# A graph layer on one core: the first part rearranged, and a sort whose last two merges stop early

## The chip, the cores and the metric

One core of a Trainium2 chip. The time is the device time of one execution in microseconds (us), and a kernel's time is the median of its runs. The trace gives one execution; its times count from the span's start.

## The reference

6250 nodes of 256 numbers and 100,000 edges (src, dst). Cut to what matters:

```python
xn = layernorm(x)
# graph part: a degree and a sum of rows over the edges
deg  = segment_sum(ones, src, n);  norm = rsqrt(1 + deg)
h    = norm * (xn @ W.T + bias)
gnn  = norm * (segment_sum(h[dst], src, n) + h)
# mixing part: linear attention with a gate
q, k, v = split(xn @ Wqkv);  k = softmax(k, over all nodes)
ctx  = k^T v per head;       out = q @ ctx
gate = sigmoid(gelu(layernorm(xn) * ln_g + ln_b) @ Wg1 + bg1) @ Wg2 + bg2)
x    = x + gnn + (out * gate) @ Wproj + bproj
# feed forward for about the half of the nodes with the largest weight
z    = layernorm(x);  w = z @ wr + br;  chosen = the 3124 largest w
x    = x + z  (and for the chosen: + w * (gelu(z @ w1 + b1) @ w2 + b2))
```

The edges reach the kernel in the order of dst. The sum needs them by src, and h[dst] is fetched row by row.

## The kernel before, in words

Node n is row n // 50 of window n % 50: 50 windows (NW) of 125 rows. An engine runs its own list of instructions in the written order and waits on semaphores; there is no scheduler. On VectorE nearly each instruction waits for the one before it (`step`).

**First part, to about 466 us.** VectorE makes from the edges row and window numbers, and counts the degrees in four chunks: `histogram(n)` first waits until TensorE has used up the chunk before (s_hist), then writes 50 comparisons with window numbers (L900) and 125 with row numbers (L904), and TensorE adds them up with 200 small matmuls (L592). The result is `deg`, from which `norm` comes (then s_normd), and a table of how many blocks of 256 edges each window needs: `first_block`, `end_block`, and `visits_due` for freeing. Each edge is packed into one key (window, row, column), and 128 x 1024 keys are sorted by a bitonic network on VectorE: a stage is a min (L975) and a max (L976). Stages within a partition for 768 of the columns come first (`early`, 36 stages, run by `lead` and then "open"), then those of the full width (9 + 10 of `local`, then the merges m = 1 to 7 over the partitions, with transposes at L998 and a sign product at L1002). Between them lie other duties of VectorE: the statistics of x (`rstd`, `nmr`, `r2`, then s_stats), `split_row`, and 25 `peek`s, each a maximum over a pair of windows of keys that TensorE has put into PSUM (`keys`; TensorE's pair i waits for peek i - 2). A peek inside the sort comes when `stages` reaches PEEK * (peeks - PEEK_FROM) - PEEK_LEAD. `stages` counts quarters of full-width stages: a stage on 768 columns counts 3, one on 1024 counts 4, and stages run by `lead` (open_keys=False) count nothing. When `stages` reaches KMAX_AT, VectorE splits the row of maxima into three bf16 parts and signals s_kmr.

ScalarE loads weights, computes the sum of each window's row (L440) for all 50 windows, then the sum of squares (L446) for all 50; x comes by SyncE in 5 loads of 10 windows (s_in0 to 4). Then it normalises each window (`scaled`), copies its transpose (`stored`) and makes the gate (`activated`, `gate_out`).

TensorE: `histogram(0)`, the transposes of the weights, `histogram(1)`, then over m = 0 to 49 `turn`, `hidden`, `keys`, `gate`, with the other two chunks ahead of m = 6 and 14 (HIST_AT). Then `main` (the rows h, of which the table in HBM is made: ScalarE `h_out`, GpSimd the subtraction L387, SyncE the stores), and from s_kmr on `keys_values` and `contexts` over 50 windows, with further `main`s in the first 17. Ahead of m = 28 (KEYS_AT) it waits for s_sortd and transposes the sorted keys (L732), of which VectorE makes columns and rows (s_tabs). After the last window it signals s_ctxd (L743).

**Second part, the gather loop.** GpSimd fetches rows of the table by column: 391 blocks of 256 edges, two gathers of 128 rows each (L403), in 23 rounds of 17 slots. It waits for s_freed for each block, and in the first round ahead of slot 14 for s_ctxd, for the last slots of `gath` also hold `qkv`. SyncE sees that a block has landed (s_arrived), waits until TensorE's count of visits reaches `visits_due`, and raises s_freed, which lets GpSimd run 15 blocks ahead; it also loads the column numbers of the next round. TensorE visits, per window w, the blocks first_block[w] to end_block[w] - 1 (`sums`, 2 matmuls L764 a visit), against a one-hot matrix that VectorE makes for each (`hots`, L1151, a ring of 8). In the same window lie turn_z, attention, up (L802), down (L812) and project (L787) on TensorE, `normed` on VectorE and the GELUs on ScalarE.

**Tail.** After the last window a search in 11 steps for the threshold, the sum for the chosen nodes and the stores.

Of the kernel before, what the change touches and what calls it, by code (L numbers as in the profile page):

```python
# [10 lines left out]
I32 = mybir.dt.int32  # L11
ALU = mybir.AluOpType
# [25 lines left out]
LAG = 2  # L38
HCH = 200
# [33 lines left out]
def gps_layer(nc, x, src, dst, W, bias, Wqkv, Wproj, bproj, ln_g, ln_b, Wg1, bg1, Wg2, bg2,  # L73
# [3 lines left out]
    with ctx:  # L77
# [205 lines left out]
        def _(sp):  # L283
# [125 lines left out]
        def _(a):  # L409
# [22 lines left out]
            a.wait_ge(s["wmain"], 16 * 9)  # L432
            for o in range(2):
                a.activation(WT[:, o, :], W_in[:, o, :], ACT.Square, accum_out=wss[:, o:o + 1]).then_inc(s["wss"], 1)
            for w in range(NW):
                if w % XCH == 0:
                    a.wait_ge(s_x[w // XCH], 32)
                if w >= SPILL:
                    a.wait_ge(s["bn"], w - SPILL + 1)
                a.activation(unused(xn)[:, w % SPILL, :], big_g[0:P, w, :], ACT.Identity, scale=-1.0 / C,  # L440
                             accum_out=mean_n[:, w:w + 1]).then_inc(s["bn"], 1)
            for w in range(NW):
                a.wait_ge(s["bn"], w + 1)
                if w >= SPILL:
                    a.wait_ge(s["bna"], w - SPILL + 1)
                a.activation(unused(h_s)[:, w % SPILL, :], big_g[0:P, w, :], ACT.Square, bias=mean_n[:, w:w + 1],  # L446
                             accum_out=var[:, w:w + 1]).then_inc(s["bna"], 1)
# [39 lines left out]
            a.wait_ge(s["bg1"], 1)  # L487
            for m in range(NW):
# [93 lines left out]
        def _(t):  # L582
# [35 lines left out]
            histogram(1)  # L618
# [128 lines left out]
            def sums(w, j, nth):  # L747
# [9 lines left out]
                with counted(t, f"sums{next(loops)}", first, end) as (q, upto):  # L757
                    made = q + (w + 1)
# [105 lines left out]
        def _(v):  # L864
# [19 lines left out]

            v.wait_ge(s["edges"], 64)
# [42 lines left out]

            v.wait_ge(s["wss"], 2)
            step(nc.vector.tensor_tensor(wun[:, :], b_col[:, :], b_col[:, :], ALU.mult))  # L930
            step(nc.vector.scalar_tensor_tensor(wss[:, :], wss[:, :], float(C), wun[:, :], ALU.mult, ALU.add))
            wss_i, wsc_i, wun_i = (of[:, :].bitcast(I32) for of in (wss, wsc, wun))
            step(nc.vector.tensor_scalar(wss_i, wss_i, 23, None, ALU.logical_shift_right))
            step(nc.vector.tensor_scalar(wss_i, wss_i, 2, None, ALU.add))
            step(nc.vector.tensor_scalar(wss_i, wss_i, 1, None, ALU.logical_shift_right))
            step(nc.vector.tensor_scalar(wsc_i, wss_i, -1.0, float(205 + TOP - 15), ALU.mult, ALU.add))
            step(nc.vector.tensor_scalar(wsc_i, wsc_i, 23, None, ALU.logical_shift_left))
            step(nc.vector.tensor_scalar(wun_i, wss_i, float(49 + 15 - TOP), None, ALU.add))
            step(nc.vector.tensor_scalar(wun_i, wun_i, 23, None, ALU.logical_shift_left))
            for o in range(2):  # L940
                step(nc.vector.tensor_scalar(W_in[:, o, :], W_in[:, o, :], wsc[:, o:o + 1], None, ALU.mult))
            nc.vector.tensor_tensor(b_col[:, :], b_col[:, :], wsc[:, :], ALU.mult).then_inc(s["wsc"], 1)

            for m in range(8):
                step(nc.vector.tensor_scalar(sign_i[:, m:m + 1], part_i[:, :], max(m - 1, 0), None, ALU.logical_shift_right))
            for m in range(8):
                if m == 0:
                    step(nc.vector.tensor_copy(sign_t[:, m:m + 1], sign_i[:, m:m + 1]))
                else:
                    step(nc.vector.tensor_scalar(sign_t[:, m:m + 1], sign_i[:, m:m + 1], 1, None, ALU.logical_shift_right))  # L950
                    step(nc.vector.tensor_tensor(sign_t[:, m:m + 1], sign_t[:, m:m + 1], sign_i[:, m:m + 1], ALU.bitwise_xor))
            step(nc.vector.tensor_scalar(sign_t[:, :], sign_t[:, :], 1, None, ALU.bitwise_and))
            step(nc.vector.tensor_copy(sign[:, :], sign_t[:, :]))
            step(nc.vector.tensor_scalar(sign[:, :], sign[:, :], -2.0, 1.0, ALU.mult, ALU.add))
# [69 lines left out]
            histogram(1)  # L1024
            v.wait_ge(s["kps"], 1)
# [16 lines left out]
            for _ in range(2):  # L1042
                peek()
# [5 lines left out]
            for _ in range(2):  # L1049
                peek()  # L1050
# [284 lines left out]
```

## Time and profile before

| | us |
|---|---|
| median of 3 runs (lowest, highest) | 1498.25 (1489.65, 1499.79) |
| the profiled execution | 1493.72 |
| its span, first to last instruction | 1492.0 |

A row's busy time is the sum of its instructions, and its idle time is what the engine waited just ahead of them. An engine that ends a wait is named after an arrow. POOL is GpSimd, DVE VectorE, ACT ScalarE, PE TensorE, SP SyncE; DVEq and the like are an engine's own queue of signals and transfers, PEld is TensorE's loading of weights, and PEclk the clock granted to TensorE as a share of full speed.

### The profile page before, as it was taken

The numbers are of one execution on the slowest core, as the hardware profiler recorded it, in microseconds if no ns is written. First come the engines' busy times: TensorE is split into PE (matmuls) and PEld (weight loads), VectorE is DVE, ScalarE is ACT, GpSimd is POOL, SyncE is SP. The second block draws the span as 40 slices with busy tenths as digits, with TensorE's granted clock in tenths as the row PEclk, the third lists the DMA queues.
The fourth block names the chain that finished last, engine by engine and source line by source line (L and its number), as shares of the span: only waits on it lengthen the run. The fifth ranks groups of instructions, "written<-read, shape, count | busy, mean of one in ns | idle before, by whom it ended". The sixth has DMA issues, their size and how long they took to land.

```text
span 1492.0 us, 29836 instructions
## 1 busy us (share of the span) xinstructions
PE 1146.9 (77%) x6606; PEld 868.8 (58%) x6607; DVE 1007.1 (68%) x3546; ACT 361.0 (24%) x1165; POOL 800.5 (54%) x851
## 2 busy tenths in 40 slices
PE   0367886789997888888777887878888777778843
PEld 0367775678885555556555555556565555555533
DVE  7888799999922666666655665656665556556657
ACT  0962354355421111111111111111111111111100
POOL 0000000154155777777777777777777777777700
PEclk9668998899999999999998998999999999999966
DMA  9000300022023444444443444444444344444305
GB/s 227 17 1 1 113 1 1 12 73 62 29 72 99 114 120 119 119 117 119 117 119 109 119 118 118 117 119 117 119 116 120 114 115 117 118 118 118 112 7 172
DMA packets 81194, 142.34 MB, mean 95 GB/s; under 512 B 30709, under 2 KB 53483, under 8 KB 80519
## 3 DMA queue, kind: packets, MB, share of 16 engines
q0 software_dynamic: 37536, 102.55, 23.8%
q1 hardware_dynamic: 28554, 24.55, 6.2%
q10 hardware_dynamic: 15054, 14.65, 3.3%
q8 instruction: 23, 0.38, 0.1%
q14 instruction: 27, 0.22, 0.0%
HBM read 126.43 MB, written 12.80 MB: 93 GB/s over the span
## 4 chain that ended last, share of the span: by engine, by line
DVE 25%; PE 23%; POOL 21%; issue 14%; DMA 9%; SPq 3%; ACT 2%; DVEq 1%; POOLq 1%; ACTq 0%
POOL gath L403 21%; DMA gath<-table,idx_stage 7%; PE bank L802 5%; PE bank L812 4%; PE bank L764 4%; DVE keyB L976 3%; DVE keyA L976 3%; DVE keyB L975 3%; DVE keyA L975 3%; DMA bg_t<-in_L_mix_bg 2%; DVE big_t L904 2%; SPq L337 2%; PE bank L779 2%; DVE big_g L1310 1%; PE bank L592 1%
## 5 line engine op out<-in xcount | busy, mean ns | idle before, releaser
L403 POOL DMA_INDIRECT gath<-table,idx_stage x782 | 748.9, 958 | 280.9 <-issue 226.0
L764 PE MATMUL bank<-gath,onehot 128*128 x880 | 272.8, 395 | 162.8 <-SPq L336 109.5
L1151 DVE TENSOR_SCALAR onehot<-iota_b,row_of,minus_row 128x128 bf16 x880 | 247.3, 334 | 133.9 <-issue 81.2
L764 PEld LDWEIGHTS bank<-gath,onehot 128*128 x880 | 84.5, 96 | 341.3 <-DVE onehot L1151 155.1
L802 PE MATMUL bank<-vv,w_sb 128*128 128x125 f32 x1600 | 212.1, 296 | 0.9 <-ACT vv L549 0.9
L802 PEld LDWEIGHTS bank<-vv,w_sb 128*128 128x128 f32 x1600 | 207.5, 213 | 2.6 <-ACT vv L549 1.7
L387 POOL TENSOR_TENSOR parts<-h_s,parts 125x256 f16<-125x256 f32 x50 | 46.8, 943 | 294.3 <-ACT parts L510 294.2
L812 PE MATMUL bank<-w_sb,keyB 128*125 128x256 f32 x800 | 181.0, 379 | 0.0
L563 ACT ACTIVATE WT<-bank,norm 125x256 f32<-125x256 f32 x50 | 23.7, 473 | 636.6 <-PE bank L771 624.9
L812 PEld LDWEIGHTS bank<-w_sb,keyB 128*125 128x125 f32 x800 | 146.3, 188 | 19.7
L555 ACT ACTIVATE keyB<-bank,b_sb 128x125 f32<-128x125 f32 x400 | 113.0, 366 | 184.4 <-PE bank L802 184.4
L1181 DVE SCALAR_TENSOR_TENSOR WT<-bank,norm,WT 125x256 f32<-125x256 f32 x50 | 24.2, 484 | 185.9 <-ACT WT L563 183.2
L592 PE MATMUL bank<-gath,big_t 125*128 125x50 bf16 x800 | 40.5, 230 | 55.6 <-DVE big_t L904 55.6
L779 PE MATMUL bank<-big_t,Wqc 128*128 (+1 forms) x400 | 72.1, 339 | 0.8 <-DVE Wqc L1247 0.8
L592 PEld LDWEIGHTS bank<-gath,big_t 125*128 125x128 bf16 x800 | 40.1, 120 | 55.9 <-DVE big_t L904 55.9
L779 PEld LDWEIGHTS bank<-big_t,Wqc 128*128 128x128 f32 x400 | 66.9, 252 | 1.3 <-DVE Wqc L1247 1.0
L904 DVE TENSOR_SCALAR big_t<-onehot 125x200 bf16<-125x200 bf16 x500 | 60.9, 216 | 0.0
L644 PE MATMUL bank<-big_t,gath 128*128 128x250 f32 x136 | 41.3, 457 | 24.3 <-DVE kpart L970 24.3
L787 PE MATMUL bank<-proj,W_in 128*125 128x256 f32 x200 | 52.9, 388 | 8.2 <-DVE W_in L1163 8.1
L691 PE MATMUL bank<-WT,big_t 128*125 128x256 f32 x200 | 52.3, 390 | 2.2 <-ACT parts L510 2.2
L699 PE MATMUL bank<-gath,big_t 128*125 128x256 f32 x200 | 51.5, 379 | 3.3 <-DVEq L991 3.3
L975 DVE TENSOR_TENSOR keyA<-keyB 128x512 f32<-128x512 f32 (+2 forms) x78 | 51.8, 664 | 2.4
(263 smaller groups left out, 1589.0 us busy)
## 6 DMA issues: line engine op xcount, KB each, us to landing
gath<-table,idx_stage POOLq DMA_INDIRECT x782, 2.7
parts<-table ACTq DMA_DIRECT2D x50, 125.0 KB
h_s<-in_x ACTq DMA_DIRECT2D x50, 125.0 KB
big_g<-in_x SPq DMA_DIRECT2D x5, 1120.0 KB
table<-parts SPq DMA_DIRECT2D x50, 112.0 KB
out<-big_g SPq DMA_DIRECT2D x10, 560.0 KB
w_sb<-in_L_ffn_w SPq DMA_DIRECT2D x2, 1024.0 KB
big_t<-w_sb SPq DMA_DIRECT2D x2, 1000.0 KB, 6.1
```

The source lines that it names most:

```text
L403: g.indirect_dma_start(out=gath[:, j, :], out_offset=None, in_=table[:, :], in_offset=bass.IndirectOffsetOnAxis(ap=idx_stage[:, j:j + 1], ...
L555: a.activation(hid[:, k, :], bank[5 + k // 4][:, (k % 4) * P:(k % 4 + 1) * P], ACT.Gelu_apprx_tanh, bias=b1_sb[:, k:k + 1]).then_inc(s["ge ...
L592: last = t.matmul(bank[3][:, 0:NW], hot_row[:, u // RUN, :, u % RUN], hot_win[:, u // RUN, :, u % RUN], start=False, stop=False, skip_grou ...
L764: last = t.matmul(bank[0][:, 0:PART], onehot_g[:, hot_slots, u * 128:(u + 1) * 128].rearrange("p a r -> p (a r)"), gath_g[:, slots, u * PA ...
L779: last = t.matmul(bank[1][:, half * P:(half + 1) * P], Wqc[:, c, half * 128:(half + 1) * 128], xnT[:, bass.ds(m, 1), c, :].rearrange("p a ...
L787: last = t.matmul(bank[3][0:P, 0:C], ogT[:, c, :], proj[:, c, :], start=c == 0, stop=c == 1)
L802: last = t.matmul(bank[5 + k // 4][:, (k % 4) * P:(k % 4 + 1) * P], w1_sb[:, c, k * 128:(k + 1) * 128], zT[:, c, :], start=c == 0, stop=c ...
L812: last = t.matmul(bank[7][0:P, 0:C], hid[:, k, :], w2_sb[:, k, :], start=k == 0, stop=k == HC - 1)
L904: last = nc.vector.tensor_scalar(hot_row[:, :, r, :], rows, float(r), None, ALU.is_equal)
L975: nc.vector.tensor_tensor(lo_out, lo_in, hi_in, ALU.min).then_inc(s["chain"], 1)
L976: nc.vector.tensor_tensor(hi_out, lo_in, hi_in, ALU.max).then_inc(s["chain"], 1)
L1151: last = nc.vector.tensor_scalar(onehot_g[:, slots, u * 128:(u + 1) * 128].rearrange("p a r -> p (a r)"), iota_b[:, :], row_of[:, bass.ds( ...
```

## The change

1. ScalarE does sums and squares per load of 10 windows instead of all sums first; the squares of W come after the third load instead of at the head.
2. VectorE's eight columns of signs are made as 8 wide operations ahead of the wait for the edges, instead of about 27 small ones behind the first histogram chunk. The scaling of W (from `wss`) moves behind the key building and two early stages.
3. The statistics go into the middle of the second histogram chunk, and s_stats is raised twice: for `rstd` and `nmr`, then for `r2`.
4. TensorE runs chunks 1, 2, 3 ahead of m = 3, 9, 15 (before: 1 ahead of the loop, 2 and 3 ahead of m = 6 and 14). VectorE has 26 instead of 16 of the 36 early stages in `lead`, laid between the chunks; peek 1 goes into chunk 2.
5. The block table comes after the remaining early stages. KEYS_AT is 24 instead of 28, PEEK_LEAD 20 instead of 12. KMAX_AT stays 297 (its formula does not hold PEEK_LEAD).
6. Merge m = 6 stops at distance 2^7 (its last seven stages go), merge m = 7 at 2^8 (its last two go). So keys are in order up to a short distance, and each window's range of blocks is widened: it starts at round(x) - 1 and ends behind round(x), where x is the count of edges up to there / 256, so that neighbours share two blocks and not one. The count of visits has 2 * m in place of m.

```diff
-PEEK_FROM, PEEK, PEEK_LEAD = 7, 17, 12
+PEEK_FROM, PEEK, PEEK_LEAD = 7, 17, 20
-HIST_AT = (6, 14)
-KEYS_AT = 28
+HIST_AT = (3, 9, 15)
+WSS_AT = 2
+KEYS_AT = 24
-LEADS = (4, 9, 16)
+LEADS = (2, 12, 17, 22, 26)
+MERGE_DOWN_TO = {6: 7, 7: 8}
...
@@ ScalarE
+            for q in range(NXL):
+                a.wait_ge(s_x[q], 32)
+                for w in range(q * XCH, (q + 1) * XCH):
...
+                for w in range(q * XCH, (q + 1) * XCH):
...
+                if q == WSS_AT:
+                    a.wait_ge(s["wmain"], 16 * 9)
...
             a.wait_ge(s["bg1"], 1)
+            a.wait_ge(s["stats"], 2)
...
@@ TensorE
-            histogram(1)
             t.wait_ge(s["wev"], 4)
...
-                    made = q + (w + 1)
+                    made = q + (2 * w + 1)
...
@@ VectorE
+            histogram(1, between=statistics)
+            lead(LEADS[0], LEADS[1])
+            peek()
+            histogram(2, between=peek)
+            peek()
             split_row(rows_h, "wtp", 1)
             v.sem_inc(s["rowsh"], 1)
+            lead(LEADS[1], LEADS[2])
             peek()
+            lead(LEADS[2], LEADS[3])
             histogram(3, between=peek)
+            peek()
+            lead(LEADS[3], LEADS[4])
+            peek()
...
+            for k, e in early[LEADS[4]:]:
+                local_stage(k, e, 0, EARLY)
...
-            step(nc.vector.tensor_scalar(til_i[:, :], scan[:, :], 1.0 / GEDGE, 0.5 / GEDGE - 0.5, ALU.mult, ALU.add))
+            step(nc.vector.tensor_scalar(til_i[:, :], scan[:, :], 1.0 / GEDGE, 0.5 / GEDGE - 1.0, ALU.mult, ALU.add))
+            step(nc.vector.tensor_scalar(til[:, :], til[:, :], 0.0, float(NBLK - 2), ALU.max, ALU.min))
-            step(nc.vector.tensor_scalar(end_block[:, :], til[0:1, :], 1.0, None, ALU.add))
+            step(nc.vector.tensor_scalar(end_block[:, :], til[0:1, :], 2.0, None, ALU.add))
...
-                for e in range(LOGF - 1, 6 if m == 7 else -1, -1):
+                for e in range(LOGF - 1, MERGE_DOWN_TO.get(m, 0) - 1, -1):
```

## Rows read from the trace of the kernel before

**Rows 1.** By stretch: us, busy us (count) of PE, PEld, DVE, ACT, POOL, PEclk, DMA, GB/s.

```profile
0.00:36.00 36.00, 0.61 (x10) 0.50 (x12) 27.56 (x193) 1.28 (x1) 2.48 (x15) 1.00 0.96 230
314.00:412.00 98.00, 97.16 (x530) 83.37 (x530) 95.61 (x114) 46.98 (x124) 32.62 (x35) 1.00 0.16 47
466.00:1418.00 952.00, 769.59 (x3985) 541.24 (x3985) 580.58 (x2143) 145.17 (x481) 722.18 (x754) 0.94 0.41 118
```

**Rows 2.** Timeline of GpSimd: start, us, instruction, in brackets idle time before it.

```profile
421.14 1.16 POOL L403 DMA_INDIRECT gath<-table,idx_stage  x1 [32.92 <-issue]
...
466.12 0.95 POOL L403 DMA_INDIRECT gath<-table,idx_stage  x1 [10.09 <-PE bank L743]
...
1417.09 0.95 POOL L403 DMA_INDIRECT gath<-table,idx_stage  x1 [0.30 <-issue]
```

**Rows 3.** GpSimd's gathers from 466 us on: shortest, median and longest in ns.

```profile
L403 POOL DMA_INDIRECT gath<-table,idx_stage x754: 942/946/1203, 466.1 to 1417.1; - x189
```

**Rows 4.** Timeline of TensorE.

```profile
314.44 1.13 PE L699 MATMUL bank<-gath,big_t 128*125 128x256 f32 x4 [3.26 <-DVEq L991]
...
412.31 1.09 PE L732 MATMUL bank<-ident,keyA 128*128 128x128 f32 x8 [0.70 <-DVEq L1114]
...
464.63 0.61 PE L743 MATMUL bank<-zeros_b,ident 128*128 128x129 f32 x4
...
513.35 0.17 PE L771 MATMUL bank<-zeros_b,ident_b 128*128 128x8 bf16 x1
...
531.23 0.17 PE L771 MATMUL bank<-zeros_b,ident_b 128*128 128x8 bf16 x1
...
1420.82 1.03 PE L764 MATMUL bank<-gath,onehot 128*128 x2 [2.85 <-SPq L336]
```

**Rows 5.** Timeline of VectorE in the first part.

```profile
41.77 0.16 DVE L930 TENSOR_TENSOR wun<-b_col 128x2 f32<-128x2 f32 x1 [6.21 <-ACT WT L434]
...
86.45 0.19 DVE L1032 TENSOR_SCALAR var<-var 125x50 f32<-125x50 f32 x1 [5.57 <-ACT h_s L446]
...
94.62 6.13 DVE L900 TENSOR_SCALAR gath<-onehot 125x200 bf16<-125x200 bf16 x50
...
166.00 0.21 DVE L1054 COPY deg<-bank 125x50 f32<-125x50 f32 x1 [4.68 <-PE bank L669]
...
205.62 0.69 DVE L975 TENSOR_TENSOR keyB<-keyA 128x512 f32<-128x512 f32 x1
...
282.62 0.68 DVE L970 TENSOR_REDUCE kpart<-bank 128x2 f32<-128x500 f32 x1
...
310.67 0.64 DVE L911 CAST rows_b<-lnb_wide 1x256 bf16<-1x256 f32 x1
...
411.51 0.68 DVE L976 TENSOR_TENSOR keyA<-keyB 128x512 f32<-128x512 f32 x1
```

**Rows 6.** VectorE by line and shape: 76 to 161 (two), 205.5 to 283, 293 to 391.

```profile
L904 DVE TENSOR_SCALAR big_t<-onehot 125x200 bf16<-125x200 bf16 x250 | 30.5, 214 | 0.0
...
L975 DVE TENSOR_TENSOR keyB<-keyA 128x384 f32<-128x384 f32 x8 | 4.5, 561 | 0.4
...
L975 DVE TENSOR_TENSOR keyA<-keyB 128x512 f32<-128x512 f32 x23 | 15.9, 691 | 0.7
...
L975 DVE TENSOR_TENSOR keyA<-keyB 128x512 f32<-128x512 f32 x22 | 19.1, 868 | 0.8
```

**Rows 7.** ScalarE by line, 40 to 90 us: count, busy us, mean ns, idle before.

```profile
L446 ACT ACTIVATE h_s<-big_g,mean_n 125x256 bf16<-125x256 f32 x50 | 24.6, 493 | 0.0
L440 ACT ACTIVATE xn<-big_g 125x256 bf16<-125x256 f32 x50 | 20.0, 400 | 0.0
```

**Rows 8.** From the page's costliest groups: TensorE's histogram matmuls, four chunks of 200.

```profile
L592 PE MATMUL bank<-gath,big_t 125*128 125x50 bf16 x800 | 40.5, 230 | 55.6 <-DVE big_t L904 55.6
```

**Rows 9.** By line in the gather loop, 466 to 1418 us: VectorE's onehots, TensorE's visits.

```profile
L1151 DVE TENSOR_SCALAR onehot<-iota_b,row_of,minus_row 128x128 bf16 x864 | 242.8, 334 | 130.6 <-issue 78.6 <-PE bank L764 45.8
...
L764 PE MATMUL bank<-gath,onehot 128*128 x878 | 271.8, 394 | 160.0 <-SPq L336 106.6 <-issue 26.1 <-DVE onehot L1151 24.1
```

More of the change, by code:

```diff
@@ L430, in unused @@
                 return of[:, :, :].rearrange("p a c -> p (a c)").bitcast(BF16).rearrange("p (a c) -> p a c", a=SPILL)
[L432 to L447, printed above, removed]
+            for q in range(NXL):
+                a.wait_ge(s_x[q], 32)
+                for w in range(q * XCH, (q + 1) * XCH):
+                    if w >= SPILL:
+                        a.wait_ge(s["bn"], w - SPILL + 1)
+                    a.activation(unused(xn)[:, w % SPILL, :], big_g[0:P, w, :], ACT.Identity, scale=-1.0 / C,
+                                 accum_out=mean_n[:, w:w + 1]).then_inc(s["bn"], 1)
+                for w in range(q * XCH, (q + 1) * XCH):
+                    a.wait_ge(s["bn"], w + 1)
+                    if w >= SPILL:
+                        a.wait_ge(s["bna"], w - SPILL + 1)
+                    a.activation(unused(h_s)[:, w % SPILL, :], big_g[0:P, w, :], ACT.Square, bias=mean_n[:, w:w + 1],
+                                 accum_out=var[:, w:w + 1]).then_inc(s["bna"], 1)
+                if q == WSS_AT:
+                    a.wait_ge(s["wmain"], 16 * 9)
+                    for o in range(2):
+                        a.activation(WT[:, o, :], W_in[:, o, :], ACT.Square, accum_out=wss[:, o:o + 1]).then_inc(s["wss"], 1)
             a.wait_ge(s["wmain"], 16 * 9)
@@ L927, in _ @@
             histogram(0)
[L929 to L954, printed above, removed]
             step(nc.vector.memset(keyA[:, :], EMPTY))
@@ L1039, in _ @@
-            inverse_sqrt(r2[:, :], nwt[:, 0, :], nwt[:, 1, :])
-            v.sem_inc(s["stats"], 1)
-            histogram(2)
-            for _ in range(2):
-                peek()
+            lead(0, LEADS[0])
+            v.wait_ge(s["wss"], 2)
+            step(nc.vector.tensor_tensor(wun[:, :], b_col[:, :], b_col[:, :], ALU.mult))
+            step(nc.vector.scalar_tensor_tensor(wss[:, :], wss[:, :], float(C), wun[:, :], ALU.mult, ALU.add))
+            wss_i, wsc_i, wun_i = (of[:, :].bitcast(I32) for of in (wss, wsc, wun))
@@ L1044, in _ @@
+            histogram(1, between=statistics)
[3 more added lines that the diff above has]
+            peek()
             split_row(rows_h, "wtp", 1)
             v.sem_inc(s["rowsh"], 1)
-            lead(LEADS[0], LEADS[1])
+            lead(LEADS[1], LEADS[2])
             peek()
+            lead(LEADS[2], LEADS[3])
             histogram(3, between=peek)
-            for _ in range(2):
-                peek()
-            lead(LEADS[1], LEADS[2])
+            peek()
@@ L1144, in hots @@
                 with counted(v, f"hots{next(loops)}", first, end) as (q, upto):
[L1145 removed]
+                    made = q + (2 * m + 1)
                     for value in (made, made % HOTS, q * GROUP):
```

64 lines of the change are left out of this document (41 added, 23 removed).

## The prediction

> **What bounds the kernel now.** I read the stretches first [rows 1]. In the gather loop (466 to 1418 us) GpSimd is busy 722 of 952 us, TensorE 770, VectorE 581, so shares do not name the limit; the gathers' own rows do. Gather 29 starts at 466.12 and gather 782 at 1417.09 [rows 2]: 753 steps of 1.263 us, against a median gather of 0.946 us and a gap of 0.30 us in front of each [rows 2, 3], 1.246 us. The difference, 12.8 us in all, is the only slack in 952 us. GpSimd is the bound of the loop, and the time is: start of gather 29, plus 951 us, plus the tail of 74 us.
>
> So the question is what starts gather 29. The first gather starts at 421.14, and 28 run; the 29th then waited 10.09 us for TensorE's L743 [rows 2], the end of the last `contexts` (s_ctxd, needed because the slots from 28 on hold `qkv`). That end is at 464.63 + 0.61 us [rows 4]. From 314.44 on TensorE does `keys_values` without a gap: 97.2 busy of 98 us [rows 1], with one wait of 0.70 us for the sorted keys at 412.31. At 314.44 it waited 3.26 us for VectorE's s_kmr (L991) [rows 4]. So the chain is: VectorE reaches the point KMAX_AT (310.67, where the row split begins, 3.7 us long) [rows 5], then 149 us of TensorE less 0.7, then the loop. The end of the sort (411.5) is only just on it.
>
> **Where KMAX_AT moves to.** I rebuild VectorE's order by durations.
>
> (a) Begin. The eight sign operations (0.2 us each) go into the wait for the edges and cost nothing. The first histogram chunk ends at 35.6 as before. The 6.21 us wait at 41.77 goes [rows 5]; key building (4.9 us) and two early stages (1.06 us each, from 0.56 + 0.55 overlapped, [rows 6]) follow, to 42.6.
>
> (b) ScalarE now works as x lands. Ten windows cost 10 x (0.400 + 0.493) = 8.9 us [rows 7]. x is 6.4 MB behind 0.8 MB of edges, and the stretch moved 230 GB/s [rows 1] over two queues; at 200 GB/s for this one, chunk 0 is there at 16 us and none is late. ScalarE: 16, 25, 34, 43 (`wss` at 44), 62 for s_bna instead of 86.3. Bounds: nothing lands before 12 (but `wmain` at 40.8 holds `wss`, so s_bna at 59.5), and 20 gives 66. I take 62.
>
> (c) VectorE: `wss` at 44.0, its block to 46.8, chunk two's first 50 + 62 comparisons (6.1 + 7.5 us, [rows 5, 6]) to 60.4, statistics (8.2 us, 86.45 to 94.62 before [rows 5]) 62 to 70.2, the other 63 comparisons to 77.8. Before, chunk two was ready at 75.9, but the statistics only at 94.6.
>
> (d) TensorE runs `histogram(1)` (10.1 us, [rows 8]) at m = 3. Steps m = 0 to 2 took 11.5 us after the statistics; with ScalarE held for the second s_stats they end at 79.3, the chunk at 89.5. VectorE has filled this with ten stages (88.4) and a peek, and waits 0.4. Chunk three 89.5 to 111.8, split, ten stages and peeks to 126.2, chunk four to 148.1, TensorE's part to 158.2. Four stages and two peeks (153.6) lie inside; about 4.7 us of wait stay, like the 4.68 before at 166.00. s_normd comes at 162.4 instead of 169.8: 7.4 us earlier, with ten more stages done.
>
> (e) Ten early stages are left instead of 20. They now look for TensorE's keys sooner (PEEK_LEAD 20); two of these waits come to 2.7 us. The 1.1 us wait for s_cntp goes, two small operations (0.4 us) come. Full-width stages begin at 187.1 instead of 205.6 [rows 5]: 18.5 us earlier.
>
> (f) But thresholds are counted in quarters of open stages. Early open stages give 3 quarters each: 60 before, 30 now. KMAX_AT is 297 as before, so it is reached at full stage (297 - 30) / 4 = 67 instead of 60. A full stage is 1.33 us uncontended: 205.62 to 282.62, less 10 peeks, 6 transposes and 3 sign products, is 61 us for 46. While GpSimd's `parts` subtractions run, the operations grow from 0.69 to 0.87 us on average [rows 6], and a stage to 1.6 to 1.9. Seven more stages at 1.75 are 12.3 us. Stage 52 comes at 273.3 by the shift; the last `keys` starts after it at 274.0 instead of 283.3 (9.3 earlier), and the subtractions move with it. Going on by those prices KMAX_AT is reached at 302.7, and `keys_values` begins at 306.5: **7.9 us earlier**. The nearest bounds: if the extra stages cost 1.33, TensorE's own path (9.3) is the limit; if (b) is at 66, 4 less. So 4 to 12.
>
> (g) The rest of the sort: nine stages go (seven in m = 6, two in m = 7), 11.3 + 2.7 us. m = 7 now falls under GpSimd's subtractions, + 3.5. The sort ends near 383. TensorE reaches m = 24 four steps of 2.29 us before m = 28: 411.6 - 9.2 - 7.9 = 394.5. The 0.7 us wait goes; VectorE stands idle 11 us. First gather near 403 instead of 421, gather 28 done near 439, then about 16 us wait for s_ctxd instead of 10. Most of what the sort saves is eaten here. Gather 29: **8.6 us earlier**.
>
> **What it adds in the loop.** Each window now ends two blocks after its rounded start and not one: visits are 389 + 2 x 50 = 489 instead of 440, 98 more matmuls and 98 more onehots of 0.334 us [rows 9]. TensorE unheld takes 17.9 us a window (513.35 to 531.23, nine visits [rows 4]); one visit more costs 0.83 (the visits there come so) to 0.98 us: 18.8. GpSimd needs 15.64 x 1.263 = 19.75. Cover stays, about 1 us a window, where L764's waits for arrivals are 106.6 us in all today [rows 9]. SP's `freed`: 15 blocks of lead, and the visit that frees a block comes 12 to 14 us later at worst, 6 blocks; only in window 1, where TensorE starts behind, a block 6 or 7 can hold the gather: 0 to 3 us, I take 1. Gathers beside onehots: if all 12.8 us of stretching came from today's 864 onehots, 98 more cost 1.5; I take 0.8. Tail: before the last block TensorE waited 2.85 us [rows 4], enough for one visit more and half a block of delay: 0.2.
>
> A rule against this change: the rows show that a gather's issue beside onehots is 942 ns at least, 946 at the median and 1203 at most [rows 3], so onehots hardly stretch it. The Trainium skill, "SBUF — State Buffer", section "SBUF: two separate sides", says that a VectorE operation in a two-port mode locks GpSimd out of writing descriptors. By that rule 98 onehots could cost up to 33 us more, by the rows 0 to 1.5; most of the trace speaks against it.
>
> **Sum.** -8.6 + 1 + 0.8 + 0.2 = -6.6 us. The profiled execution (1493.72, span 1492.0) would be 1487.1; the median of the runs shown is 1498.25, and 1498.25 - 6.6 = 1491.6. I say 1491.5. The case's own range: 1486 to 1496.
>
> **Rivals.**
> 1. The start of the gathers decides, because s_ctxd comes earlier than I think: the wait of 10.09 us vanishes and gather 29 follows 35 us after a first gather at 403, 27.7 us earlier; half of that, 14 to 28 us, is 1470 to 1484. For it: 33 us of VectorE work or waits go ahead of the sort's end. Against: TensorE is busy 97.2 of 98 us and nothing of `keys_values` gets shorter. 0.18; some 0.15 of it beyond 1%.
> 2. The extra visits make TensorE or GpSimd slower than 19.75 us a window. Place: the window loop; point: one visit more costs over 1.9 us in all, or every onehot blocks a gather for its 0.334 us (98 x 0.334 = 33 us, 1498.25 - 8.6 + 33 = 1522). TensorE 0.5 us over the gathers in 48 windows gives 1513. For it: TensorE's visits often wait for onehots (24.1 us [rows 9]), and 0.98 us a visit is VectorE's pace. Against: the 1 us of cover. 0.12.
> 3. The change does nothing: KMAX_AT 4 us earlier and 3 us held in window 1; 1496 to 1501. 0.18.
> My own case: 0.52.
>
> A few runs of this kernel tell about 1% (15 us) from no change. Faster by more 0.15, within 0.76, slower 0.09 (rival 2's milder half stays within). The range for 8 in 10 takes my case, rival 3, the nearer part of rival 1 and rival 2's begin: 1479 to 1504.
>
> **What would show it.** Statistics between 60 and 70 us inside chunk two; full-width stages from about 187; L991's release near 306; the sort's end near 383 with VectorE idle some 11 us ahead of L732; gather 1 near 403, gather 29 near 457.5 after a wait for L743 of about 16 us; 489 visits; 1.263 us a gather. I am wrong if gather 29 comes before 450 or after 463, if GpSimd's gaps grow past 0.30 us through the loop, or if L764's waits for arrivals vanish.

## The result, and the profile after

| | before | changed |
|---|---|---|
| median (lowest, highest), us | 1498.25 (1489.65, 1500.03) | 1488.3 (1485.61, 1490.97) |
| span of the profiled execution | 1492.0 | 1488.4 |

The ratio is 0.9948, with a 95% interval of 0.9928 to 0.9968: 0.5% faster, which counts as within 1%. The forecast was 1491.5. The medians lie 10.0 us apart, the spans of the two profiled executions 3.6: the one before was 4.5 us faster than its median, the changed one 1.9 us slower.

The stretches of the changed kernel that answer to [rows 1], with the same columns (us, busy us and count of PE, PEld, DVE, ACT, POOL, PEclk, DMA share, GB/s):

```profile
0.00:36.00 36.00, 0.70 (x12) 0.60 (x14) 29.30 (x202) 21.47 (x93) 2.48 (x15) 1.00 0.97 235
304.00:400.00 96.00, 96.00 (x514) 82.17 (x515) 79.50 (x88) 45.58 (x120) 36.44 (x34) 0.97 0.16 48
457.00:1419.00 962.00, 781.00 (x4081) 524.80 (x4081) 611.87 (x2238) 144.72 (x481) 727.33 (x754) 0.97 0.40 116
```

Its GpSimd timeline answers to [rows 2]. The gathers begin 18.2 us earlier, but gather 29, behind a wait of 19.2 us and no longer 10.1 for the contexts (L746, before L743), only 9.0 us earlier, and the last gather is no earlier at all:

```profile
402.98 1.16 POOL L405 DMA_INDIRECT gath<-table,idx_stage  x1 [22.40 <-issue]
...
457.13 0.95 POOL L405 DMA_INDIRECT gath<-table,idx_stage  x1 [19.22 <-PE bank L746]
...
482.81 0.94 POOL L405 DMA_INDIRECT gath<-table,idx_stage  x1 [0.99 <-SPq L341]
...
486.75 0.94 POOL L405 DMA_INDIRECT gath<-table,idx_stage  x1 [1.74 <-SPq L341]
...
542.46 0.94 POOL L405 DMA_INDIRECT gath<-table,idx_stage  x1 [2.90 <-SPq L341]
...
1417.61 0.95 POOL L405 DMA_INDIRECT gath<-table,idx_stage  x1 [0.30 <-issue]
```

The first part on VectorE and TensorE: the two timelines answer to [rows 5] and [rows 4]. The row split is at 300.62 (before 310.67), TensorE takes its signal at 303.89 (before 314.44), and VectorE is done with the sort at 381.1 and then stands:

```profile
43.59 0.16 DVE L1012 TENSOR_TENSOR wun<-b_col 128x2 f32<-128x2 f32 x1 [1.00 <-ACT WT L450]
...
61.43 0.19 DVE L1033 TENSOR_SCALAR var<-var 125x50 f32<-125x50 f32 x1 [0.18 <-ACT h_s L445]
...
156.80 0.21 DVE L1060 COPY deg<-bank 125x50 f32<-125x50 f32 x1 [4.83 <-PE bank L672]
...
184.25 0.69 DVE L960 TENSOR_TENSOR keyB<-keyA 128x512 f32<-128x512 f32 x1
...
300.62 0.28 DVE L923 CAST rows_b<-lnb_wide 1x256 bf16<-1x256 f32 x1
...
379.97 1.15 DVE L961 TENSOR_TENSOR keyA<-keyB 128x512 f32<-128x512 f32 x1
...
395.28 0.69 DVE L1127 COPY keyB<-bank 128x512 f32<-128x512 f32 x1 [14.15 <-PE bank L735]
```

```profile
288.87 0.37 PE L723 MATMUL bank<-ident,kmax 128*1 128x128 f32 x1 [3.19 <-DVE kmax L972]
...
303.89 2.07 PE L702 MATMUL bank<-gath,big_t 128*125 128x256 f32 x4 [3.64 <-DVEq L976]
```

The balance of the two spans, from gather 29 to the end: start -9.0; holds by s_freed beyond the usual gap +4.4 (4.7 against 0.3); the gathers' own durations and usual gaps over those 753 steps +5.1; from the last gather's start to the end 70.8 instead of 74.9, -4.1. Sum -3.6, the 1492.0 - 1488.4 seen.

### The profile page after: what moved, and what is told of

Its sections match the earlier page's. It is cut to its first block, busy times and chain, and to the rows that moved or that the text cites. A ratio compares the mean times of both kernels' runs of the same rounds, so it can differ in the third digit from the quotient of the medians.

```text
span 1488.4 us, 30493 instructions
## 1 busy us (share of the span) xinstructions
PE 1159.1 (78%) x6704; PEld 852.9 (57%) x6705; DVE 1027.4 (69%) x3612; ACT 360.8 (24%) x1165; POOL 809.8 (54%) x851
## 4 chain that ended last, share of the span: by engine, by line
PE 33%; DVE 26%; issue 14%; POOL 13%; DMA 5%; SPq 3%; DVEq 3%; ACT 3%; POOLq 0%; ACTq 0%
POOL gath L405 13%; PE bank L767 6%; PE bank L805 5%; PE bank L815 5%; DMA gath<-table,idx_stage 4%; PE bank L702 3%; PE bank L705 3%; DVE onehot L1159 3%; DVE big_t L916 3%; DVE keyA L961 2%; PE bank L694 2%; DVE keyB L961 2%; SPq L339 2%; DVE keyB L960 2%; DVE keyA L960 2%
## 5 line engine op out<-in xcount | busy, mean ns | idle before, releaser
L1159 DVE TENSOR_SCALAR onehot<-iota_b,row_of,minus_row 128x128 bf16 x978 | 277.3, 331 | 217.5 <-PE bank L767 110.5
L767 PE MATMUL bank<-gath,onehot 128*128 x978 | 301.0, 395 | 147.5 <-SPq L338 72.4
L767 PEld LDWEIGHTS bank<-gath,onehot 128*128 x978 | 93.9, 96 | 351.5 <-DVE onehot L1159 176.5
L389 POOL TENSOR_TENSOR parts<-h_s,parts 125x256 f16<-125x256 f32 x50 | 50.7, 1021 | 280.7 <-ACT parts L514 280.3
L805 PE MATMUL bank<-vv,w_sb 128*128 128x125 f32 x1600 | 198.4, 284 | 1.1 <-ACT vv L553 1.1
L805 PEld LDWEIGHTS bank<-vv,w_sb 128*128 128x128 f32 x1600 | 191.4, 199 | 3.0 <-ACT vv L553 1.7
L782 PE MATMUL bank<-big_t,Wqc 128*128 (+1 forms) x400 | 62.6, 306 | 0.8 <-DVE Wqc L1255 0.8
L782 PEld LDWEIGHTS bank<-big_t,Wqc 128*128 128x128 f32 x400 | 56.7, 218 | 1.5 <-DVE Wqc L1255 1.0
L960 DVE TENSOR_TENSOR keyB<-keyA 128x512 f32<-128x512 f32 (+2 forms) x78 | 51.3, 658 | 2.6
```

The costliest lines, as they stand in the source:

```text
L767: last = t.matmul(bank[0][:, 0:PART], onehot_g[:, hot_slots, u * 128:(u + 1) * 128].rearrange("p a r -> p (a r)"), gath_g[:, slots, u * PA ...
L782: last = t.matmul(bank[1][:, half * P:(half + 1) * P], Wqc[:, c, half * 128:(half + 1) * 128], xnT[:, bass.ds(m, 1), c, :].rearrange("p a ...
L805: last = t.matmul(bank[5 + k // 4][:, (k % 4) * P:(k % 4 + 1) * P], w1_sb[:, c, k * 128:(k + 1) * 128], zT[:, c, :], start=c == 0, stop=c ...
L960: nc.vector.tensor_tensor(lo_out, lo_in, hi_in, ALU.min).then_inc(s["chain"], 1)
L1159: last = nc.vector.tensor_scalar(onehot_g[:, slots, u * 128:(u + 1) * 128].rearrange("p a r -> p (a r)"), iota_b[:, :], row_of[:, bass.ds( ...
```

## The experiments

The table has one row per kernel: times of GpSimd's first, 29th and last gather (us from the span's start), holds beyond the gap of 0.30 us after gather 29, mean duration of the gathers from the 29th on, and the rest of the span behind the last gather's start. "Ratio" is against the kernel before on the same chip.

| kernel | median | ratio (95%) | first | 29th | last | holds | mean | rest |
|---|---|---|---|---|---|---|---|---|
| before | | | 421.1 | 466.1 | 1417.1 | 0.3 | 0.959 | 74.9 |
| changed | 1488.3 | 0.9948 (.9928-.9968) | 403.0 | 457.1 | 1417.6 | 4.7 | 0.966 | 70.8 |
| e1_narrow | 1484.18 | 0.9932 (.9910-.9954) | 402.0 | 456.2 | 1409.7 | 0 | 0.961 | 74.5 |
| e2_wide | 1501.15 | 1.0052 (1.0034-1.0071) | 421.2 | 466.0 | 1425.1 | 2.7 | 0.965 | 74.6 |
| e3_peek14 | 1469.44 | 0.9842 (.9825-.9860) | 392.2 | 437.1 | 1393.7 | 2.9 | 0.963 | 74.0 |
| e4_probe | 1524.44 | one run | 404.6 | 458.7 | 1450.1 | 36.8 | 0.965 | 72.5 |
| e10_narrow14 | 1468.7 | 0.9820 (.9795-.9845) | 402.1 | 437.7 | 1390.4 | 1.4 | 0.958 | 75.8 |
| e11_before14 | 1500.89 | 1.0028 (1.0012-1.0044) | 425.6 | 472.6 | 1425.7 | 0 | 0.961 | 74.3 |
| e12_before14 | 1486.35 | 0.9940 (.9922-.9957) | 428.6 | 463.8 | 1412.5 | 0 | 0.957 | 76.1 |
| **e9_peek12** | **1459.63** | **0.9766 (.9747-.9785)** | 392.1 | 427.4 | 1385.3 | 3.0 | 0.965 | 72.8 |

Theory A throughout: the time is the start of gather 29, plus 753 gathers of 1.26 us, plus the rest; and gather 29 is set by the row split (KMAX_AT), with the start of the gathers off the path. Its rivals stand with each run.

### Do the cut merges gain, and do the wide ranges cost?

e1_narrow is the changed kernel with finished merges and the old ranges; e2_wide is the kernel before with the wide ranges alone.

```diff
e1_narrow, against the changed kernel
-MERGE_DOWN_TO = {6: 7, 7: 8}
+MERGE_DOWN_TO = {7: 7}
...
-                    made = q + (2 * w + 1)
+                    made = q + (w + 1)
...
e2_wide, against the kernel before
-                    made = q + (w + 1)
+                    made = q + (2 * w + 1)
...
-            step(nc.vector.tensor_scalar(end_block[:, :], til[0:1, :], 1.0, None, ALU.add))
+            step(nc.vector.tensor_scalar(end_block[:, :], til[0:1, :], 2.0, None, ALU.add))
...
```

> The changed kernel with the merges finished as before (eight more full-width stages) and each window's range of blocks as narrow as before (440 visits). Theory A (TensorE's keys_values sets gather 29, the extra visits cost in the loop): the sort ends some 13 us later, near 394, just as TensorE comes to m = 24; gather 29 stays at 457 to 459; the holds of GpSimd by the freeing of blocks (0.99, 1.74 and 2.90 us) go, so the step from gather 29 to 782 goes from 960.5 back to about 952 to 956; the tail is again 74 to 75 us, since TensorE idles longer ahead of the last block. Span 1484 to 1488. Theory B (the unfinished merges bring the gain): slower than the changed kernel by some 10 us or more.

> The kernel before with nothing but the wider ranges (489 visits), its sort as it was. Theory A: first part unchanged (gather 29 at 466), GpSimd is held in the first windows for 3 to 6 us in all, the tail is about 4 us shorter because TensorE's last waits are short and its clock is up; span 1490 to 1496. Theory C (onehots block the gathers' descriptors, 0.33 us each for 98 more): the step from gather 29 to 782 grows by 30 us and the span is above 1515. Theory D (the growth of the gathers' durations by 5 us in the changed kernel belongs to the visits): the mean gather is 964 ns here too; if it is a matter of which VectorE operations of a window happen to meet a gather, it may be anything from 955 to 968.

Taking the cut merges away costs nothing: gather 29 comes at 456.16, 1 us earlier than in the changed kernel, because VectorE's 14.15 us of standing idle fill with stages; 2.02 us of it are left. The wide ranges cost more than I wrote (1499.7 as span, 1490 to 1496 said, and the shorter tail expected did not come): with everything ahead of gather 29 unchanged (465.98 against 466.12), the last gather of e2_wide is 8.0 us later, by 2.3 us of holds more and 4.5 us of longer gathers and the rest in gaps. The 7.2 to 1501.15 from the 1493.97 of the kernel before on that chip agree. The step from gather 29 to the last grew by 8.2 us and not by 30, so theory C is out. So part 6 of the change, cut merges and wide ranges together, gained nothing in this kernel: with PEEK = 17 the other parts alone (e1_narrow) are worth 0.68%, all of them 0.52%, two figures whose intervals overlap.

### Is it KMAX_AT that sets the time?

```diff
e3_peek14, against the changed kernel
-PEEK_FROM, PEEK, PEEK_LEAD = 7, 17, 20
+PEEK_FROM, PEEK, PEEK_LEAD = 7, 14, 20
-KEYS_AT = 24
+KEYS_AT = 28
```

> The changed kernel with the peeks 14 quarter stages apart instead of 17 (KMAX_AT then is 246 instead of 297, stage 54 instead of 67) and KEYS_AT 28. Theory A (VectorE's peeks and the KMAX_AT point pace TensorE, and its end of keys_values sets gather 29): the last keys of TensorE some 18 to 20 us earlier (near 252), s_kmr near 282 instead of 304, gather 29 near 437 to 440 instead of 457, span 1468 to 1472. Theory B (the end of the sort, or the start of the gathers, sets the end): no gain, since the sort ends where it did or a little later and TensorE's m = 28 is reached no earlier than m = 24 was.

Theory A holds, with a span of 1467.7, 0.3 us under its range. Peeks now come every 3.5 and not every 4.25 full stages, KMAX_AT falls from 297 to 246, TensorE takes the row split's signal at 283.9 instead of 303.9, and gather 29 moves by the same 20.0 us:

```profile
437.12 0.94 POOL L405 DMA_INDIRECT gath<-table,idx_stage  x1 [9.97 <-PE bank L746]
```

Two constants, PEEK and the KEYS_AT that goes with it, give more than the whole rearrangement. The wait of 9.97 us for the contexts says that TensorE still sets it, and how much is left until the 28 gathers do. This wait is only 9 us shorter than in the changed kernel, because the first gather moved as well, from 402.98 to 392.18: TensorE now comes to the sorted keys at 383.35 instead of 394.20.

### What does a VectorE operation cost a gather?

e4_probe put 40 comparisons of the onehot's form and then 40 sums of two f32 inputs (125 x 256) behind `hots(0)`; e8_probe put them the other way round ahead of it.

```diff
e8_probe, against the changed kernel
+            spin = keyB[:, 0:64].bitcast(BF16)
+            for _ in range(40):
+                step(nc.vector.tensor_tensor(keyB[0:P, 256:512], keyB[0:P, 512:768], keyB[0:P, 768:1024], ALU.add))
+            for _ in range(40):
+                step(nc.vector.tensor_scalar(spin, iota_b[:, :], row_of[:, 0:1], minus_row[:, 0:1],
+                                             ALU.subtract, ALU.is_equal))
             hots(0, bounds_of(0))
```

> The changed kernel with 80 more operations on VectorE in its wait for s_ctxd, beside the gathers from 403 to 438 us: first 40 of the onehot's form (128 x 128 bf16 from a constant tile and two scalars), then 40 sums of two 125 x 256 f32 tiles into a third. Theory C (a two-port operation locks GpSimd out): the gathers beside the first 40 stretch from 0.95 to 1.1 us or more each. Theory E (sums with two inputs in SBUF stretch the gathers, onehots do not): those beside the first 40 stay at 0.95, those beside the second 40 go to 1.07 to 1.2 us. If neither: all at 0.95. The span stays within 2 us, as the gathers after all wait for s_ctxd at 457.

> The changed kernel with 80 more VectorE operations between the first gather and the first onehot, where VectorE else waits 50 us: first 40 sums of two f32 inputs (125x256), then 40 comparisons of the onehot's form (128x128 bf16). Theory A (two-input sums delay a gather's issue, onehots do not): the gathers beside the first 40 take 1.05 to 1.10 us, those beside the second 40 0.94 to 0.96, as do those beside nothing. Theory B (it depends on VectorE being busy at all): both groups over 1.0 us. The span changes by less than 3 us against the changed kernel.

In e4_probe I had overlooked that `hots(0)` makes one onehot more than its ring of 8 holds. That last one waits for TensorE's first visit, so the probe began at 461.17, behind the contexts, and VectorE left the path's next step 34.7 us late:

```profile
460.71 0.54 DVE L1159 TENSOR_SCALAR onehot<-iota_b,row_of,minus_row 128x128 bf16 x2 [51.91 <-PE bank L767]
461.17 16.32 DVE L1246 TENSOR_SCALAR keyB<-iota_b,row_of,minus_row 128x128 bf16<-128x128 bf16 x40
477.52 18.36 DVE L1249 TENSOR_TENSOR keyB<-keyB 125x256 f32<-125x256 f32 x40
```

```profile
517.07 0.94 POOL L405 DMA_INDIRECT gath<-table,idx_stage  x1 [33.25 <-SPq L341]
```

Of the 34.7 us 33.3 stood at GpSimd as one wait: in the first windows next to no cover exists, which fits the place of the three holds of the changed kernel, 482 to 543. (Its 1524.44 us is no result on the price of an operation.) But the gathers ahead of that wait have the price: 13 of them beside the comparisons took 0.94 or 0.95 us, and the three wholly beside the sums, from 479.99 on, 1.07 or 1.08.

e8_probe, on a slower chip of which more below, gave the same price over more gathers. VectorE's rows and, under them, GpSimd's beside them:

```profile
400.87 18.36 DVE L1243 TENSOR_TENSOR keyB<-keyB 125x256 f32<-125x256 f32 x40 [0.43 <-DVE row_of L1133]
419.27 16.50 DVE L1245 TENSOR_SCALAR keyB<-iota_b,row_of,minus_row 128x128 bf16<-128x128 bf16 x40
```

```profile
406.64 0.99 POOL L405 DMA_INDIRECT gath<-table,idx_stage  x1 [0.30 <-issue]
407.94 1.08 POOL L405 DMA_INDIRECT gath<-table,idx_stage  x1 [0.31 <-issue]
409.32 1.07 POOL L405 DMA_INDIRECT gath<-table,idx_stage  x1 [0.30 <-SPq L341]
...
417.60 1.08 POOL L405 DMA_INDIRECT gath<-table,idx_stage  x1 [0.30 <-issue]
418.98 1.07 POOL L405 DMA_INDIRECT gath<-table,idx_stage  x1 [0.30 <-issue]
420.36 0.95 POOL L405 DMA_INDIRECT gath<-table,idx_stage  x1 [0.30 <-issue]
421.61 0.95 POOL L405 DMA_INDIRECT gath<-table,idx_stage  x1 [0.30 <-issue]
```

From 407.9 to 419 nine gathers of 1.07 or 1.08 us; from 420.36, beside the comparisons, 0.94 or 0.95, as beside nothing. So a onehot costs a gather nothing that can be seen, and sums of two SBUF inputs, back to back, cost 0.12 us a gather. The Trainium skill, "SBUF — State Buffer", section "SBUF: two separate sides", has a VectorE operation with two SBUF inputs share a port pair with GpSimd when GpSimd reads SBUF, and says that the loser "fully blocks". That such sums meet a gather, both probes bear out; they show no block for the length of the operation, for the sums took 0.46 us each, two or more met each gather, and it grew by 0.12.

Then why do 98 more onehots lengthen the gathers? In the loop I matched every gather of 1.12 us or more with the VectorE operations beside it. There are 14 of them before, and 10 to 19 in the four other kernels with narrow ranges (e1, e10, e11, e12); there are 42 in the changed kernel, and 33 to 40 in the four others with wide ones (e2, e3, e4, e9). The additional ones of the changed kernel lie beside L1178 and L1181 (`mixed`, 12, none with narrow ranges) and beside L1193 to L1201 (`normed`, 12, against 3 before): operations of two inputs that run in every window. Beside the onehots the wide ranges add nothing to what VectorE runs, so they must change when these chains run. That the chains lie closer to one another, and that this makes them dearer, is my reading; I have not tried it alone.

### Together with the narrow ranges, and how far down PEEK goes

```diff
e6_narrow14 and e10_narrow14, against e1_narrow
-PEEK_FROM, PEEK, PEEK_LEAD = 7, 17, 20
+PEEK_FROM, PEEK, PEEK_LEAD = 7, 14, 20
-KEYS_AT = 24
+KEYS_AT = 32
e5_peek11, against the changed kernel: PEEK = 11, KEYS_AT = 35
e9_peek12, against the changed kernel: PEEK = 12, KEYS_AT = 33
```

> The changed kernel with PEEK = 11 and KEYS_AT = 35. Theory A (gather 29 follows the later of two times: 149 to 153 us behind the row split, or 28 gathers behind the first one): KMAX_AT is 195, the last keys come once more earlier by up to 17 us, the last context ends near 420, and gather 29 is bound by the end of the sort: first gather near 390 to 392, gather 29 at 425 to 428 with no wait for the contexts; 1457 to 1462 us. Theory B (the peeks themselves are what costs, and fewer places for them leave TensorE's keys late): no gain over PEEK = 14, 1468 to 1472. Theory C (the loop gives it back, since TensorE starts a window behind): holds of over 3 us, 1463 to 1468.

> The changed kernel with finished merges and narrow ranges (440 visits), PEEK = 14 and KEYS_AT = 32. Theory A: the sort ends some 11 us later than with the merges cut (near 392), first gather near 402.5, gather 29 near 438 instead of 437.1; the loop then has no holds (2.9 us fewer) and some 3 us less of stretched gathers: 1464 to 1467 us. Theory B (the cut merges are what makes gather 29 early): 29 at 448 or later, 1476 or more.

> The kernel of e6_narrow14 once more, because in that call every kernel, the one before too, took some 46% longer, with ScalarE standing still for 12 to 21 us wherever gathers ran. Ahead of the gathers it did as expected (row split's signal used at 284.96 us, first gather at 402.70). On a chip without those halts, theory A: gather 29 near 438, no holds, 1464 to 1467 us. Theory B (the cut merges are what makes gather 29 early): gather 29 at 448 or later, 1476 or more.

> The changed kernel (cut merges, wide ranges) with PEEK = 12 and KEYS_AT = 33. Theory A (gather 29 is the later of TensorE's last context and 28 gathers behind the first): KMAX_AT is 212, keys_values begins near 275 and the contexts end near 428; the sort ends at 382 to 386, the first gather comes at 391 to 394, so both ways give 428 to 430 for gather 29, some 8 us earlier than e3_peek14. With its loop (2 to 3 us of holds, 0.963 us a gather) 1460 to 1464 us, against 1469.44 and 1468.7 of e3_peek14 and e10_narrow14. Theory B (with the peeks packed closer VectorE reaches TensorE's keys too early and waits, so that the sort ends later by as much): first gather at 397 or later, 1465 to 1470.

e5 to e8 ran on one chip on which all kernels took 46% longer: the kernel before 2178.62 us, e5_peek11 2149.08, e6_narrow14 2151.33, e7_before14 2182.2, e8_probe 2176.68. Their whole times say nothing on the theories, but ahead of the first gather their traces are like those of the other chips (row split's signal in e6_narrow14 at 284.96, first gather at 402.70), and those parts count. The last section shows the difference. In e5_peek11 the signal came at 269.2 and the sorted keys were waited for until 387.2, with a first gather at 397.2. The sort ended at 387.1, 4 us later than with PEEK = 12 below (383.2), and its gathers began 5.1 us later, so 11 looks worse than 12; its whole time on an ordinary chip was not measured. e7_before14, at a ratio of 1.0025, already showed what e11_before14 shows below.

e10_narrow14 did what A says, 1.7 us above its range: gather 29 at 437.72 behind a wait of 0.63 us. It is now bound by the 28 gathers behind a first one at 402. That is where the cut merges begin to be worth something: e9_peek12, which keeps them, starts its gathers at 392.12; TensorE takes the row split's signal at 274.19, waits only 0.60 us for the sorted keys at 383.30, and is done at 424.8, so gather 29 has no wait:

```profile
392.12 1.17 POOL L405 DMA_INDIRECT gath<-table,idx_stage  x1 [43.39 <-issue]
...
424.85 0.94 POOL L405 DMA_INDIRECT gath<-table,idx_stage  x1 [0.30 <-PE bank L746]
...
427.35 0.95 POOL L405 DMA_INDIRECT gath<-table,idx_stage  x1 [0.30 <-issue]
...
456.67 0.94 POOL L405 DMA_INDIRECT gath<-table,idx_stage  x1 [1.64 <-SPq L341]
```

```profile
274.19 1.03 PE L702 MATMUL bank<-gath,big_t 128*125 128x256 f32 x4
...
383.30 1.09 PE L735 MATMUL bank<-ident,keyA 128*128 128x128 f32 x8 [0.60 <-DVEq L1122]
```

At 1459.63 us, just below A's range, it beats both kernels, 2.3% under the one before. Against e10_narrow14 it pays 5 us in the loop for wide ranges and gets 10 for the earlier first gather. PEEK = 12 with finished merges was not run; as the sort of e10_narrow14 ended at 393.0 and its gathers, which already set gather 29, began at 402, I estimate that it would gain next to nothing over e10_narrow14.

### Does the kernel before gain from PEEK = 14 as well?

```diff
e7_before14 and e11_before14, against the kernel before
-PEEK_FROM, PEEK, PEEK_LEAD = 7, 17, 12
+PEEK_FROM, PEEK, PEEK_LEAD = 7, 14, 12
e12_before14, besides
-KEYS_AT = 28
+KEYS_AT = 37
```

> The kernel before with PEEK = 14 alone. Theory A: the row split comes 18 to 20 us earlier (near 291), the contexts end near 446, but the sort still ends at 411.5 and the first gather comes at 421, so gather 29 is at 456.3 without a wait for the contexts: 10 us earlier than before, 1482 to 1486 us; so the rearrangement, worth 8 us with PEEK = 17, is worth some 15 with 14. Theory B (the gain of PEEK = 14 is one of the changed kernel's order only): same as before, 1492 to 1496.

> The kernel of e7_before14 once more, for the same reason. Ahead of the gathers it showed keys_values begun at 295.9 (before: 314.4), the sorted keys waited for 19.8 us and a first gather at 422.5. Theory A: gather 29 near 457.6 without a wait for the contexts, 8.5 us earlier than before: 1484 to 1488 us. Theory B (the wait for the sorted keys is only moved into TensorE's path: 29 stays at 463 or later): 1491 to 1496. Theory C (PEEK = 14 gives the kernel before all 20 us): 1473 to 1476.

> The kernel before with PEEK = 14 and KEYS_AT = 37 instead of 28, so that TensorE does nine more windows of keys_values before it needs the sorted keys. Theory A (in e11_before14 the 20 us of KMAX_AT were lost because TensorE stood at m = 28 for the sorted keys and had 22 windows of 2.29 us left behind them): no wait for the keys, contexts end near 446 to 450, first gather 421 to 425, gather 29 at 457 to 461 bound by the 28 gathers: 1485 to 1490 us, so the change is worth 18 to 25 us with PEEK = 14 on both sides. Theory B (VectorE or ScalarE is late for another reason): gather 29 at 466 or later, 1496 to 1501.

In e11_before14 none of my three ranges held; it was slower than before by 0.28%. Theory B had the mechanism, the wait moved into TensorE's path, but not its price. TensorE has its signal 16.6 us earlier (297.86), but stands at m = 28 for the sorted keys:

```profile
415.94 1.97 PE L732 MATMUL bank<-ident,keyA 128*128 128x128 f32 x8 [19.24 <-DVEq L1114]
```

Behind that wait there are still 22 windows of 2.29 us, and gather 29 comes at 472.59. I had treated the sort's end and the row split as two ends of which the later counts; they are two entries into one TensorE queue, and what stands behind KEYS_AT has to be added to the later of them. With KEYS_AT = 37 (e12_before14) the wait is gone, the contexts end at 452.1, and gather 29 comes at 463.82, bound by the 28 gathers behind a first one at 428.58: 1486.35 us, in A's range, though contexts and gathers came 2 to 4 us later than A's places for them (the profiled execution took 1490.44). The first gather is 7.4 us later than before. The sort itself is hardly longer (163.0 us of full-width operations, before 162.2); its last stage is 6.0 us later (417.5 for 411.5) because its first is 6.4 us later (212.0 for 205.6). Ahead of it VectorE waits 1.5 us longer for `wss` (7.68 instead of 6.21; 5.54 to 7.09 in the other kernels with the old order), 2.1 longer for `deg` (6.8 instead of 4.7, in e7, e11 and e12 alike) and 1.9 more for TensorE's keys at the peeks, of which one more lies there. The other 1.5 us is TensorE, which comes to the sorted keys that much after they are done. With PEEK = 14 the change is worth the step from 0.9940 (e12_before14) to 0.9842 (e3_peek14), or to 0.9820 without part 6 (e10_narrow14), with PEEK = 17 from 1 to 0.9948; these ratios come from different chips.

## Why the prediction was right, by its steps

The path was named rightly: row split, TensorE's `keys_values` and `contexts`, 28 gathers off the path, then GpSimd's pace. (TensorE's part is 150.8 us by [rows 4], 314.44 to 465.24, and not 149; only its change enters the sum.) Most times of the first part met theirs within 2.5 us: `wss` 43.6 (44.0), statistics 61.4 (62), the wait for `deg` 4.83 (4.7), first gather 402.98 (403), gather 29 457.13 (457.5).

- **Full-width stages** began at 184.25, not 187.1. The two peeks' waits in (e) were 1.8 us and not 2.7, and `deg` came at 156.8, not 158.2.
- **Row split, (f).** 300.62 instead of 302.7. That the counting of quarters eats about half of the 21 us gained was right; the gain at TensorE was 10.5 us instead of 7.9. I had not seen that TensorE would wait 3.19 us for the last peek's maximum at 288.87. It did not delay the signal, which TensorE again awaited (3.64 us), but it has a part in the next point.
- **From there to gather 29** 153.2 us instead of 151.7, so that the start was 9.0 us earlier for 8.6 said. The sum had no term for TensorE's clock. After the two stands, 3.19 us before 288.87 and 3.64 before 303.89, the clock granted from 304 to 308 was 0.50, the lower level of 1.2 GHz, and 0.85 over the first 16 us; before, with the one stand of 3.26 us, it was 1.00. The first four matmuls took 2.07 us instead of 1.13 [rows 4], and by the second `main` TensorE was 2.5 us behind the pace of before. Less the 0.70 us wait for the sorted keys, which went as said, that leaves 1.8 us, near the 1.5 measured.

```profile
304.00:320.00 16.00, 16.00 (x72) 13.19 (x73) 15.62 (x20) 7.01 (x18) 4.26 (x5) 0.85 0.14 40
```

- **The sort, (g).** Both the description of the change and step (g) say that merge m = 7 loses two stages. The kernel before already stopped it after distance 2^7 (the diff's `6 if m == 7` is where the range ends, and 6 itself isn't in it), so one stage went, eight in all. By step (g)'s own prices this is 1.3 us at the sort's end. It ended at 381.1 (383 said), and as VectorE then stood 14.15 us (11 said), the error lay where nothing hangs on it.
- **Holds: mis-sized.** 1 us taken, 0 to 3 as bounds; 4.7 measured. I allowed one block to hold in window 1. There were three, at 482.81, 486.75 and 542.46, so TensorE was still behind 85 us after its late start; e2_wide, e3_peek14 and e9_peek12 show 2.7 to 3.0 us of them, the kernels with narrow ranges 0 to 1.4.
- **Gathers beside more work: mis-sized.** 0.8 taken and 1.5 as the bound; 5.1 measured. The bound came from giving all of the stretching to the onehots. They had next to none of it (e8_probe, e4_probe). What e2_wide shows is that the wide ranges lengthen the gathers by 4.5 us, and most of the additional long ones lie beside `mixed` and `normed`; why is open.
- **The rest behind the last gather: mis-sized**, +0.2 said, -4.1 in the one execution, and of the wrong sign. TensorE waited 0.63 us for the last block instead of 2.85 [rows 4], and up()'s 32 matmuls took 3.84 us instead of 6.64. These rows are from the kernel before and the changed one:

```profile
1417.00:1430.00 13.00, 9.32 (x43) 7.95 (x44) 6.43 (x25) 2.46 (x8) 0.95 (x1) 0.61 0.07 20
```

```profile
1417.00:1430.00 13.00, 10.10 (x60) 7.56 (x59) 9.02 (x35) 3.00 (x10) 1.25 (x2) 1.00 0.09 26
```

The clock granted was 0.61 before and 1.00 after. This goes with the ranges: in the 13 us behind the last gather it was 0.61 to 0.74 in the five kernels with narrow ranges, whose TensorE stood 2.20 to 3.62 us ahead of its last visit, and 0.74 to 1.00 in the five with wide ones, which stood 0.59 to 1.39. The rest was 74.3 to 76.1 us in the first and 70.8 to 74.6 in the second, 2.2 us less in the mean, so about half of the 4.1 belongs to the change and the other half to that execution.

A gather's step was 1.276 us and not the 1.263 named as a sign; the 489 visits came, and TensorE's waits for arrivals shrank to 72.4 us but did not vanish. Terms of 8 us that went wrong in the loop stand against 0.4 us of a better start and 4.3 us of the rest. Measured by the two traces the gain was 3.6 us for 6.6 said, by the medians 10.0; that the forecast met the time within 3.2 us is partly luck.

Of the rivals, the first (the start of the gathers decides) fell with the wait of 19.22 us. The second has the right direction and the wrong mechanism: the loop does become slower, but TensorE is not slower than GpSimd's windows, for it still waits 72.4 us for arrivals; it only starts behind, which makes the three holds, and onehots don't block. The third, nothing gained, was near: it needed 4 us off the row split's gain and 3 us of holds, and only the holds came.

## What to carry to other kernels

When a wait ahead of the bound grows from 10 to 19 us, as here at gather 29, the part just improved is off the path, and the size of the wait is what may be gained by moving its releaser alone; more only if the other path moves as well. Here PEEK from 17 to 14, with KEYS_AT set to match, gave 20 us and left 10 of the wait of 19, because the first gather came 11 us earlier too, and 14 to 12 gave the other 10. A threshold that counts work done (PEEK, KMAX_AT, KEYS_AT) has to be set anew when the work before it changes, and a wait inside a queue is priced with all that stands behind it in that queue. An expedient such as an unfinished sort is worth only what the path lets through: it gained nothing with PEEK = 17 and is part of the best kernel with PEEK = 12.

## What the runs showed of the hardware

- Sums of two f32 inputs in SBUF, back to back on VectorE, lengthen the issue of a gather of 128 rows from 0.95 to 1.07 us; comparisons on 128 x 128 bf16 don't (0.94 to 0.95). e8_probe and e4_probe agree, on two chips.
- In the changed kernel two stands of TensorE, 3.19 and 3.64 us between 285.7 and 303.9, were followed by 4 us at a granted clock of 0.50 (1.2 GHz), in which four f32 matmuls of 128 x 256 took 2.07 us instead of 1.13. The same 2.07 followed a wait for the row split's signal of 3.75 to 4.99 us in e1, e3, e4, e6, e8 and e12; it stayed at 1.13 after 3.26 us in the kernel before, 3.41 in e2, and also after 3.79 in e11, so the length of that wait does not tell it alone.
- One chip took 2178.62 us for the kernel that takes 1493.97 to 1496.27 on three others. Same kernel, same groups of ScalarE (count, busy us, mean ns, idle before), first e10_narrow14, then e6_narrow14 on that chip:

```profile
L559 ACT ACTIVATE keyB<-bank,b_sb 128x125 f32<-128x125 f32 x400 | 113.3, 367 | 183.4 <-PE bank L805 183.4
```

```profile
L559 ACT ACTIVATE keyB<-bank,b_sb 128x125 f32<-128x125 f32 x400 | 107.9, 379 | 794.0 <-remote 758.3 <-PE bank L805 35.8
```

The instructions take about the same time (367 and 379 ns). What differs are the waits, for something that the trace does not name. They begin with the gathers. Beside the first 28 of them (402.7 to 437.7) ScalarE stood twice in steps that otherwise come every 2.29 us, and kept time again soon after GpSimd stopped:

```profile
406.23 0.38 ACT L522 ACTIVATE xn<-bank 125x256 f32<-125x256 f32 x1 [1.85 <-PE bank L705]
...
417.64 0.38 ACT L522 ACTIVATE xn<-bank 125x256 f32<-125x256 f32 x1 [10.74 <-remote]
...
439.36 0.38 ACT L522 ACTIVATE xn<-bank 125x256 f32<-125x256 f32 x1 [21.07 <-issue]
...
447.02 0.38 ACT L522 ACTIVATE xn<-bank 125x256 f32<-125x256 f32 x1 [1.63 <-PE bank L705]
```

A gather took 0.95 us there too. Which resource the gathers hold on that chip, no run here tells.
